# Half of a shared up product moved from behind the expert loop to in front of it, with a buffer of its own

## What is computed

```python
out = jnp.einsum('boi,bih->boh', agg_w, x) + agg_b[:, :, None]      # conditioned mix, gives xt
scores = softmax(xt @ router_w + router_b) + router_bias            # top 2 of 16, by groups
h = jax.nn.silu(xt @ w1 + b1) * (xt @ w2 + b2)                      # per expert, 128 wide
y = y + ge[:, None] * (h @ w3 + b3)
z = jax.nn.silu(xt @ sw1 + sb1) * (xt @ sw2 + sb2) @ sw3 + sb3      # shared, 256 wide
x = x + y + z
```

## Time and profile before

| what | us |
|---|---|
| median of 3 runs (lowest, highest) | 284.51 (283.58, 286.88) |
| span of the profiled execution | 282.6 |
| PE busy in it | 253.3 |
| PE weight loads | 163.0 |
| DVE busy | 150.1 |
| POOL busy | 126.0 |
| ACT busy | 78.6 |

### The profile page before, as it was taken

One profiled execution on the slowest core, in us unless ns is written; L12 is line 12 of the kernel. 1 busy time (PEld: TensorE's weight loads), 2 busy tenths in 40 slices (PEclk: granted clock), 3 DMA queues, 4 the chain that ended last, 5 costly groups with the idle time before them and its releaser, 6 DMA issues.

```text
span 282.6 us, 4281 instructions
## 1 busy us (share of the span) xinstructions
PE 253.3 (90%) x1092; PEld 163.0 (58%) x1093; DVE 150.1 (53%) x314; ACT 78.6 (28%) x169; POOL 126.0 (45%) x204
## 2 busy tenths in 40 slices
PE   7959889899999859999999889889988979999975
PEld 6826667688864436677775455545555544444421
DVE  0497988569799763344333322332233130179894
ACT  2213455303164002333433232223322221000400
POOL 7673445310111456565656556565656565000160
PEclk9977999999999999999999999999999999999999
DMA  7996876882639359533443343434344433799963
GB/s 224 328 402 217 296 249 205 319 328 121 223 113 420 137 157 369 178 116 119 141 133 121 117 112 107 124 103 148 111 119 140 139 124 118 241 390 388 395 255 148
DMA packets 20699, 57.91 MB, mean 205 GB/s; under 512 B 2533, under 2 KB 2533, under 8 KB 20428
## 3 DMA queue, kind: packets, MB, share of 16 engines
q1 hardware_dynamic: 15084, 39.89, 39.2%
q0 software_dynamic: 5600, 17.83, 19.7%
HBM read 40.94 MB, written 17.30 MB: 206 GB/s over the span
## 4 chain that ended last, share of the span: by engine, by line
PE 38%; issue 26%; POOL 18%; DVE 12%; POOLq 3%; DMA 2%; ACT 0%
PE psum L560 36%; POOL late_region L486 12%; DVE r L959 3%; POOL from_slot L483 3%; DVE xT L1189 2%; POOL to_slot L493 2%; DVE xT L954 2%; DVE xT L928 2%; PE psum L603 2%; DVE xT L969 1%; POOL expert_rows L497 1%; DMA late_region<-xt_rows,from_slot 1%; DMA xT<-cond_pack 1%; DVE mix_bias L956 1%; POOLq L480 1%
## 5 line engine op out<-in xcount | busy, mean ns | idle before, releaser
L560 PE MATMUL psum<-wexp,r 128*128 x272 | 70.2, 387 | 2.1 <-issue 1.2
L560 PEld LDWEIGHTS psum<-wexp,r 128*128 128x128 f32 x272 | 47.1, 190 | 28.9 <-issue 22.8
L928 DVE TENSOR_TENSOR r<-psum,ebias 128x256 f32<-128x256 f32 x34 | 14.4, 425 | 82.5 <-PE psum L560 82.5
L486 POOL DMA_INDIRECT late_region<-xt_rows,from_slot x36 | 36.7, 1019 | 28.5 <-POOL from_slot L483 25.3
L497 POOL DMA_INDIRECT expert_rows<-late_region,to_slot x34 | 34.0, 1001 | 30.1 <-POOL to_slot L493 28.3
L560 PE MATMUL psum<-wexp,xt_sb 128*128 x68 | 36.7, 621 | 7.9 <-issue 7.9
L560 PE MATMUL psum<-xT,shared_sb 128*128 128x512 f32 x64 | 28.0, 593 | 0.8 <-issue 0.8
L871 ACT ACTIVATE late_region<-psum 128x512 f32<-128x512 f32 x34 | 20.3, 597 | 29.5 <-PE psum L560 29.5
L865 ACT ACTIVATE r<-r 128x128 f32<-128x128 f32 x34 | 10.5, 309 | 60.2 <-DVE r L928 60.2
L706 PE MATMUL psum<-ident,late_region 128*128 128x128 f32 x144 | 22.3, 277 | 3.6 <-DMA late_region<-xt_rows,from_slot 3.5
L1145 DVE COPY r<-psum 128x512 f32<-128x512 f32 x36 | 24.6, 684 | 1.5 <-PE psum L706 1.3
(11 more groups left out here) (175 smaller groups left out, 327.7 us busy)
## 6 DMA issues: line engine op xcount, KB each, us to landing
wexp<-expert_pack SPq DMA_DIRECT2D x16, 768.0 KB, 5.2
wexp<-expert_rows SPq DMA_DIRECT2D x8, 1024.0 KB, 13.0
xt_rows<-xt_sb SPq DMA_DIRECT2D x16, 256.0 KB, 2.5
x_early<-x SPq DMA_DIRECT2D x2, 1024.0 KB, 9.0
late_region<-x SPq DMA_DIRECT2D x2, 1024.0 KB, 13.7
ebias<-expert_bias SPq DMA_DIRECT2D x1, 2048.0 KB, 7.2
out_dram<-x_early SPq DMA_DIRECT2D x8, 256.0 KB, 9.8
shared_sb<-shared_pack SPq DMA_DIRECT2D x1, 1536.0 KB, 16.7
```

The lines of the kernel that those rows point to most:

```text
L486: nc.gpsimd.indirect_dma_start(out=xg[:, slot, :], out_offset=None, in_=xt_dram[:, :], in_offset=bass.IndirectOffsetOnAxis(ap=from_slot[:, ...
L560: return nc.tensor.matmul(dst, lhsT, rhs, start=start, stop=stop)
L928: return nc.vector.tensor_tensor(dst, a, b, op)
```

## The change

`shared_up(2, 0)` is issued by PE in front of the expert loop, behind the down product of tile 6, with a wait for four sums (`z_ready` at least 4), since it now writes banks 6 and 7, which the down products of tiles 2 and 3 used. ACT's silu of it stands in front of ACT's expert steps, DVE's hidden product behind the transposed rows of expert tile 1. PE's step 1 waits for that hidden product. `gs_third` gets memory of its own. What was run inside `shared_up(2, 0)` at the end of the loop now runs inside `shared_up(2, 1)`. The banks of the three up products left behind the loop are renamed. The scratch memory of the dynamic DMAs is 8192 bytes in each partition instead of the default 16384.

```diff
@@ -159,8 +159,7 @@
         spare = xT[:, 0, :, :].rearrange("p c n -> p (c n)")[:, TOKENS // 2:]
         x_again = ([xT[:, 1, u, :] for u in range(GT)] + [xt_sb[:, u * DIM:(u + 1) * DIM] for u in range(2)]
                    + [spare[:, u * DIM:(u + 1) * DIM] for u in range(2)])
-        gs_third = wexp_flat[:, NG * TOPK * GT * DIM:NG * TOPK * GT * DIM + IB * GN].rearrange(
-            "p (i n) -> p i n", i=IB)
+        gs_third = sb("gs_third", [P, IB, GN])
 
         ident = sb("ident", [P, P])
@@ -275,7 +274,7 @@
         GATE_BANKS = (4, 2, 3, 5)
 
-        UP_BANKS = (0, 2, 6, 0, 0, 2, 0, 2)
+        UP_BANKS = (0, 2, 6, 0, 6, 0, 2, 0)
         DOWN_BANKS = (4, 5, 6, 7, 2, 3, 4, 5) + (4, 5, 6, 7) * (NG - EARLY)
         J_ACT = 8
         J_DVE = 22
@@ -694,6 +693,8 @@
                           start=(j == 0), stop=(j == TOPK * NT - 1))
             last.then_inc(dispatch_done, 1)
             shared_down(1, range(1, GT - 1))
+            pe.wait_ge(z_ready, GT)
+            shared_up(2, 0)
 
             pe.wait_ge(tables_ready, 1)
@@ -737,6 +738,7 @@
                 up(b, e, 0)
                 if n == 1:
                     pe.wait_ge(z_ready, EARLY * GT)
+                    pe.wait_ge(up_ready, EARLY * IB + 1)
                 if n >= 1:
                     hidden_transposed(1 - b, i)
                 up(b, e, 1).then_inc(h_done, 1)
@@ -776,9 +778,8 @@
 
             last_expert = expert_of(tiles - 1)
             pe.wait_ge(xgT_ready, tiles + 2)
-            shared_up(2, 0, between={(0, 1): lambda: hidden_transposed(1, tiles),
+            shared_up(2, 1, between={(0, 1): lambda: hidden_transposed(1, tiles),
                                      (0, 2): lambda: down(1, last_expert, tiles, tiles_less_2)})
-            shared_up(2, 1)
             shared_up(3, 0)
             shared_up(3, 1)
             pe.wait_ge(y_ready, tiles)
@@ -883,6 +884,7 @@
                 for u in range(2):
                     act_step(p * 2 + u, u, (2 * q + u - 1) % RING, freed[u])
 
+            shared_silu(2, [0])
             act_pair(0, 0, (None, None))
             act_pair(1, 1, (None, None))
             act_pair(2, 0, (None, 16))
@@ -905,7 +907,7 @@
                             act_pair(p, q, (turn - 16 if q == 0 else turn, turn))
             hidden_transposed(1, tiles)
             result(1, 1, tiles, count_of(act, N_SCATTERED + 2))
-            shared_silu(2)
+            shared_silu(2, [1])
             shared_silu(3)
 
             act.wait_ge(rows_loaded[LAST], 16 * TOPK)
@@ -1162,6 +1164,7 @@
             rows_transposed(0, 1)
             shared_sum(1, [GT - 1])
             rows_transposed(1, 2)
+            shared_hidden(2, [0])
             with dve.Fori(0, SURE) as p:
                 dve_pair(p)
             pairs = count_of(dve, N_PAIRS)
@@ -1194,7 +1197,7 @@
                     if k < ks[-1] or g >= EARLY:
                         link(ins)
 
-            shared_hidden(2)
+            shared_hidden(2, [1])
             add_rows(0)
             add_rows(1)
             shared_hidden(3)
@@ -1209,7 +1212,7 @@
     import concourse.bacc as bacc
     from concourse.bass_utils import run_bass_kernel_spmd
 
-    nc = bacc.Bacc("TRN2", target_bir_lowering=False, num_devices=1)
+    nc = bacc.Bacc("TRN2", target_bir_lowering=False, num_devices=1, dynamic_dma_scratch_size=8192)
     a = {n.removeprefix("L0_").removeprefix("cond_"): np.asarray(v) for n, v in inputs.items()}
     cond, b2 = np.asarray(inputs["cond_128"]), a["b2"]
     _, out_c, in_c, _ = a["weight"].shape
```

## The result

| | before | changed |
|---|---|---|
| median of 4 runs each (lowest, highest), us | 284.04 (282.96, 286.88) | 292.0 (289.53, 293.54) |
| ratio of the times, 95% interval | | 1.0297 (1.0235 to 1.036) |
| span of the profiled execution, us | 282.6 | 291.0 |

The changed kernel is 3% slower. The forecast was 288.1, with a range that ended at 289.8: the direction was right, the size too small. The profiled spans differ by 8.4 us, and the steps of the forecast make up 3.6. Some executions of a kernel are disturbed and a few per cent longer: the medians count all of them, the ratios leave the disturbed ones out, and of two experiments whose profile fell in such an execution (the shift taken back, the half product placed) only stages are read, no spans.

The account below looks back on a forecast made before the run. POOL was taken to pace the expert loop, no single engine the whole span. Span 282.6 + 4.1 front - 3.0 tail + 2.5 clock = 286.2, plus 1.9 to the median, gave 288.1 us; range 285.2 to 289.8.

Parts of the forecast that it names:

- The front delay: Start of expert loop: the moved product makes POOL take up gather 7 late by 4.1 us (3.9 to 4.3).
- 4.2 us push everything behind them on PE: Before PE's first transposes: 2.6 us of the 6.9 us product fill the hole, the rest delays PE's later work by 4.2.
- The scratch: POOL's indirect DMAs: halving the descriptor memory costs nothing, since no POOL wait in the trace was put down to descriptor room.
- Rival 4: POOL's indirect DMAs: scratch too small, POOL stalls once more, up to 4.4 us on the forecast, 292.5 us; chance 0.04.
- the last scatter is 4.1 us late: End of expert loop: POOL cannot win back its delay, so last scatter, row loads and first added row come 4.1 later.
- The last scatter near 242.7: Sign at the end of POOL's loop: last scatter issued near 242.7 us, against 238.62 before.
- the first added row near 253.9: Sign in DVE's tail: first added row near 253.9 us, against 249.75 before.
- The tail: Behind the loop: PE released 3.0 us earlier (2.0 to 3.0), but a lower clock costs 2.5 (1.7 to 3.4).
- PE's release: Tail: DVE's sums let PE's last four down products start 3.0 us earlier (2.0 to 3.0), 268.4 instead of 271.43.
- The fall of the clock: Tail: after 6.0 us idle, PE's last down products begin at 1.2 GHz, costing 2.5 us (1.7 to 3.4).
- Rival 1: Tail: PE's clock stays at 2.4 GHz, span 283.7 us, a time of 285.6; chance 0.20.
- rivals 2 and 3: Loop: POOL wins the delay back, 281.5 us, chance 0.07. Tail: little gain, low clock at its longest, 290.0 us, chance 0.09.

Follow-up runs that it names:

- the shift taken back: Changed kernel with sixteen small warm-up matmuls issued as three wide and five small, PE's later code 32 instructions earlier; median 290.75 us (4 runs).
- the half product placed: Kernel moving only the product's w1 half, scratch 12288, with two warm-up groups made wide (24 instructions fewer); 280.82 us, ratio 0.9926 to the kernel before.

## Why the prediction was right and wrong

**The front delay: mechanism right, size wrong.** It was to be 4.1 us (3.9 to 4.3) and measured 2.57, or 2.0 to 2.1 against executions whose clock fell in the hole. The forecast's own steps up to PE's first transposes hold: the product takes 7.03 us (forecast 6.9), and the transposes come 8.53 us behind the first gather (95.49 to 104.02) instead of 4.41, 4.1 later. The failed step is "4.2 us push everything behind them on PE". The old trace has two waits there that the pushed PE no longer meets. PE's timeline before, steps 0 and 1:

```profile
104.94 1.99 PE L560 MATMUL psum<-wexp,r 128*128 x8 [0.84 <-DVE x_early L928]
...
108.81 0.30 PE L719 MATMUL psum<-ident,r 128*128 128x128 f32 x1 [0.58 <-DVE r L928]
```

With them 0.84 and 0.35 us of idle time go (the second is 0.23 in the trace after), and from the first transposes to those of step 1 it takes 7.33 us (104.02 to 111.35) instead of 8.81, 1.5 less. POOL is late by the rest. The rule that it can't be won back in the loop held: from the 8th issue on nothing came back but for the pauses told above.

**The scratch: costed at nothing, cost 1.25.** Rival 4 had the mechanism, once, with at most 4.4 us and a chance of 0.04. "No wait of POOL in the trace is put down to room for descriptors" was read from a trace with the larger memory; that can't show what a smaller one does.

**A step that wasn't there: the place of the code, 6.4 us.** It is the largest part of the loss, and it alone takes the time out of the range: without it the measured 292.0 would be 285.6, inside. The step that failed is "the last scatter is 4.1 us late": counted from the first gather it came 10.2 us late (152.09 against 141.93), by 2.6 at the front, 1.2 in the loop and 6.4 behind it. The forecast counted what the moved instructions do and not that they move what stands behind them. A hint stood in the trace: "issue" idle of 0.81 us at the jump out of the loop, and instruction transfers beside it.

**The last scatter near 242.7** was thus wrong (247.58), and the first added row near 253.9 too (258.77), while their distance is as forecast: 11.2 us.

**The tail: right.** PE's release was to be 3.0 us earlier (2.0 to 3.0). Counted from the last scatter it comes at 29.73 us (247.58 to 277.31) instead of 32.81, 3.1 earlier (2.0 earlier than in two executions of kernels with nothing moved, where it came at 31.8). No wait of DVE for a silu, 5.50 us for the eight additions, an idle time of 5.90 (6.0), a granted clock of 0.57 and 10.6 us (10.5) for the last four down products are all there. The fall of the clock was to cost 2.5 (1.7 to 3.4); it costs 2.6 on PE, and keeping it up gave 2.1. Rival 1, by which the clock would stay, is out, and rivals 2 and 3 too. What spoke for rival 1, that holes of 2.59 and 2.11 us had not brought the clock down, was one execution's: behind the same hole at the loop's start it fell in four kernels of six.

With every term as measured and the place of the code added, the forecast's sum would have been 282.6 + 2.6 + 1.3 + 6.4 - 3.1 + 2.6 = 292.4, near the span of 291.0, whose prologue was 1.2 shorter. Without the 6.4 the terms come to +3.4, where the forecast had +3.6. That is luck: the front was put 1.5 us too high and the scratch 1.3 too low, and the two misses hide each other.

## What to carry to other kernels

When work is moved ahead of something that waits, fit its size to the hole (here 2.6 us free and 7 us put in), and walk the waits behind it: each wait that the pushed engine no longer meets makes the delay smaller. Treat the place of code as part of a change: where an engine jumps out of a loop, compare the "issue" idle time there before and after, and if it has grown by microseconds, shift the code (24 instructions less were enough here) before judging the change. What PE no longer does in a tail can cost it its clock; here a dozen matmuls of no use in the gap kept it.

## What the runs showed of the hardware that was not expected

- A shift of PE's instruction list by 17 or 33 instructions lengthened the pause at a jump out of a loop from 0.8 to 3.2 and 4.1 to 4.3 us, one by 153 did not; the longer pause also brought the clock from 2.4 to 1.2 GHz, for 3.1 us more on the matmuls behind it.
- The scratch of the indirect DMAs ran out once for 8192 bytes, at the 57th of 70, for 1.25 us; for 4096 at the 29th and the 50th, for 0.6 us each; not at all for 12288 and 16384.
- Waits that are long met cost PE time where nothing hides them: with 120 and 153 such instructions at its start its first matmul began at 14.55 and 18.09 us, before at 1.59. That is 0.11 us each in both. Thirty-three of them in PE's hole cost nothing: the first transposes came 4.3 us behind the first gather, as before.
- How long PE stood does not by itself say whether its clock falls. At the start of the loop, with the same work on both sides, it stayed up over 2.59 and 2.61 us and fell around 2.52, 2.55, 2.62 and 2.63 us, for 0.5 us more to the eighth issue. In the tail it stayed up over 2.08 to 2.13 us in four kernels (1.95 us for the four records behind it) and fell around 2.20 and 2.25 us (2.97 and 2.60). A gap above 2.1 us was not safe here, and one trace in which the clock stays does not show that it will in the next.
